# Maxima of the last attention: ScalarE copies half of each bank, VectorE scans both halves together, and a router step of one thread is placed earlier on VectorE

## What is computed

```python
q = jnp.einsum('btd,hdk->bhtk', hidden_states, Wq) + bq[None, :, None, :]
k = jnp.einsum('btd,hdk->bhtk', hidden_states, Wk) + bk[None, :, None, :]
scores = jnp.einsum('bhtk,bhsk->bhts', q, k) * scale
weights = jax.nn.softmax(scores, axis=-1)
out = jnp.einsum('bhts,bhsk->bhtk', weights, v)
```

## Time and profile before

| | |
|---|---|
| runs, median of 3 | 3894.77 us (3893.24 to 3896.06) |
| the profiled execution | 3885.22 us |
| its span | 3883.4 us |
| TensorE matmul, busy | 3146.7 us (81%) |
| VectorE, busy | 2438.9 us (63%) |
| ScalarE, busy | 1662.9 us (43%) |
| GpSimd, busy | 607.5 us (16%) |

### The profile page before, as it was taken

How to read it: one execution, slowest core, us unless ns; L and a number is a source line. 1 busy time by engine, 2 the same in 40 slices (tenths; PEclk the granted TensorE clock), 3 DMA queues, 4 the chain that set the end, 5 groups by cost and what they waited for, 6 DMA issues and landing times.

```text
span 3883.4 us, 43741 instructions
## 1 busy us (share of the span) xinstructions
PE 3146.7 (81%) x16174; PEld 1595.0 (41%) x16174; DVE 2438.9 (63%) x4576; ACT 1662.9 (43%) x2458; POOL 607.5 (16%) x425
## 2 busy tenths in 40 slices
PE   3568769996799868997699868998689977996688
PEld 1134424553245433553245432554235532464145
DVE  4636876478656876568656775568755786534442
ACT  3425515464345624465155634456154642532231
POOL 2001101301022100311023010321013110211030
PEclk8578869998899878998799978998799987997696
DMA  3130244303441243302542152502443124412261
GB/s 111 69 109 1 56 146 127 101 20 100 120 142 48 48 149 109 112 18 73 142 141 69 24 149 70 160 28 54 142 120 104 30 83 133 135 58 62 59 199 46
DMA packets 201351, 355.91 MB, mean 92 GB/s; under 512 B 32994, under 2 KB 124962, under 8 KB 194914
## 3 DMA queue, kind: packets, MB, share of 16 engines
q1 hardware_dynamic: 201137, 353.11, 31.8%
HBM read 302.74 MB, written 49.66 MB: 91 GB/s over the span
## 4 chain that ended last, share of the span: by engine, by line
PE 57%; DVE 23%; DMA 7%; ACT 5%; issue 4%; POOL 2%; SPq 1%; ACTq 0%; DVEq 0%; POOLq 0%
PE PS L1805 6%; DVE MX L1596 6%; PE PS L1828 6%; PE PS L1832 6%; PE PS L1659 5%; PE PS L1667 5%; PE PS L1103 4%; PE PS L1773 3%; DMA UU<-k_scratch 3%; DVE U L898 2%; PE PS L1784 2%; DVE U L891 2%; PE PS L1154 2%; POOL D L1404 2%; PE PS L1238 1%
## 5 line engine op out<-in xcount | busy, mean ns | idle before, releaser
L1404 POOL TENSOR_TENSOR D<-D,GW 128x512 f32<-128x512 f32 x320 | 445.6, 1393 | 1451.7 <-ACT D L1477 1215.6
L783 ACT ACTIVATE U<-U 128x2048 f32<-128x2048 f32 x256 | 487.9, 1909 | 183.2 <-DVE U L891 97.6
L1645 DVE SCALAR_TENSOR_TENSOR D<-D,PS 128x512 f32<-128x512 f32 x336 | 228.4, 680 | 394.8 <-ACT D L1481 279.6
L1477 ACT ACTIVATE D<-PS 128x512 f32<-128x512 f32 x336 | 200.0, 595 | 594.5 <-PE PS L1828 594.5
L1805 PEld LDWEIGHTS PS<-WST,D 128*128 128x128 f32 (+1 forms) x2688 | 354.0, 198 | 173.1 <-DVE D L1650 103.3
L1805 PE MATMUL PS<-WST,D 128*128 128x128 f32 (+1 forms) x2688 | 380.8, 286 | 30.8 <-DVE D L1650 30.6
L1832 PE MATMUL PS<-XT,WST 128*128 128x512 f32 (+1 forms) x672 | 372.8, 637 | 32.5 <-DVE D L1645 31.6
L898 DVE SCALAR_TENSOR_TENSOR U<-PP,RD,QB 128x512 f32<-128x512 f32 x512 | 363.8, 776 | 46.2 <-ACT QB L780 27.4
L1103 PE MATMUL PS<-U,resident 128*32 128x512 f32 x2048 | 302.4, 670 | 104.2 <-ACT U L783 104.2
L1828 PE MATMUL PS<-XT,WST 128*128 128x512 f32 (+1 forms) x672 | 369.7, 633 | 16.8 <-ACT D L1481 10.0
L1596 DVE TENSOR_REDUCE MX<-PS 128x2 f32<-128x1024 f32 x256 | 299.8, 1219 | 114.8 <-PE PS L1751 114.8
(11 more groups left out here) (345 smaller groups left out, 3917.3 us busy)
## 6 DMA issues: line engine op xcount, KB each, us to landing
GW<-gates_scratch SPq DMA_DIRECT2D x320, 256.0 KB, 4.2
WST<-in_pairs_dram SPq DMA_DIRECT2D x336, 192.0 KB, 2.4
U<-band_scratch SPq DMA_DIRECT2D x32, 1280.0 KB, 7.5
UU<-in_w_dram SPq DMA_DIRECT2D x64, 512.0 KB, 7.2
UU<-pad_scratch SPq DMA_DIRECT2D x8, 1792.0 KB
UU<-q_scratch SPq DMA_DIRECT2D x24, 384.0 KB
UU<-k_scratch SPq DMA_DIRECT2D x24, 384.0 KB
e_scratch<-D SPq DMA_DIRECT2D x8, 1024.0 KB, 4.5
```

Of the source, the lines that this page charges most:

```text
L783: e.activation(ring(i), ring(i), ACT.Gelu).then_inc(S["act"], 1)
L1404: e.tensor_tensor(AV[:, n % 3, :], AV[:, n % 3, :], GW[:, p // 2 % GWS, p % 2, :], ALU.mult).then_inc(S["gated"], 1)
```

## The change

Three things change. First, a step of the score pass is one bank and not two, so there are 64. ScalarE copies the upper 256 columns of the bank to SBUF (`MXH`, eight slots). VectorE then runs a `tensor_tensor_scan` with `max` as both operations over the lower 256 columns in PSUM and the copied 256 columns: element i of the result is the maximum of everything up to i in both, and the last element is the maximum of the bank. After four banks (one head) one `tensor_copy` takes the four last elements into `MX3`. Second, the start numbers and `TURN` are new, and with them thread A's L938, L939 and L944 stand earlier on VectorE. Third, the transposes of the gates wait for all 64 scans and not for all but the last step.

```diff
@@ b_act
+            for k in range(64):
+                yield
+                e.wait_ge(S["s1_3"], at("s1_3", b, k + 1))
+                if k == 0:
+                    e.wait_ge(S["q_out3"], at("q_out3", b, 16))
+                    e.wait_ge(S["k_out3"], at("k_out3", b, 32))
+                if k >= 8:
+                    e.wait_ge(S["mx3"], at("mx3", b, k // NT - 1))
+                e.activation(MXH[:, k % 8, :], PZ(k % NT)[:, T // 2:], ACT.Copy).then_inc(S["half3"], 1)
@@ b_dve
-            for k in range(32):
-                yield
-                hd, j = k // 2, 2 * (k % 2)
-                e.wait_ge(S["s1_3"], at("s1_3", b, k + 1))
-                e.tensor_reduce(MX3[:, j:j + 2, hd], PSall[:, 4 + j:6 + j, :], AX.X, ALU.max).then_inc(S["max3"], 1)
-            yield
-            e.wait_ge(S["max3"], at("max3", b, 32))
+            for k in range(64):
+                yield
+                hd, j = k // NT, k % NT
+                e.wait_ge(S["half3"], at("half3", b, k + 1))
+                e.tensor_tensor_scan(MXH[:, k % 8, :], PZ(j)[:, 0:T // 2], MXH[:, k % 8, :], GONE, ALU.max, ALU.max).then_inc(S["max3"], 1)
+                if j == NT - 1:
+                    e.wait_ge(S["max3"], at("max3", b, k + 1))
+                    e.tensor_copy(MX3[:, :, hd], MXH[:, NT * (hd % 2):NT * (hd % 2) + NT, T // 2 - 1]).then_inc(S["mx3"], 1)
+            yield
+            e.wait_ge(S["mx3"], at("mx3", b, NH))
@@ b_pe
-            for k in range(32):
-                yield
-                hd, j = k // 2, 2 * (k % 2)
+            for k in range(64):
+                yield
+                hd, j = k // NT, k % NT
...
-                if k >= 2:
-                    e.wait_ge(S["max3"], at("max3", b, k - 1))
-                for x in range(2):
-                    last = e.matmul(PZ(j + x), QS3[:, hd, P * (j + x):P * (j + x) + P], KS3[:, hd, :], start=True, stop=True)
-                last.then_inc(S["s1_3"], 1)
-            yield
-            e.wait_ge(S["max3"], at("max3", b, 31))
+                if k >= 4:
+                    e.wait_ge(S["max3"], at("max3", b, k - 3))
+                e.matmul(PZ(j), QS3[:, hd, P * j:P * j + P], KS3[:, hd, :], start=True, stop=True).then_inc(S["s1_3"], 1)
+            yield
+            e.wait_ge(S["max3"], at("max3", b, 64))
@@ the table
-TURN = 421.20
+TURN = 412.60
```

More of the change, by code:

```diff
@@ L171, in laid_out @@
     return dict(x=w("L0_attn_x"), consts=packed(CONSTS + MASKS), resident=packed(RESIDENT), passing=packed(PASSING), last=packed(LAST), pairs=wst.reshape(PAIRS, P, 3 * P), w1=w1)
-TURN = 421.20
+TURN = 412.60
 STARTS = {
     "a_act": (
[8 rows of a table removed]
[8 rows of a table added]
     ),
     "a_dve": (
[9 rows of a table removed]
[9 rows of a table added]
     ),
     "a_pe": (
[11 rows of a table removed]
[11 rows of a table added]
     ),
     "a_pool": (
-        1.68, 20.05, 273.64,
+        1.68, 20.05, 265.09,
     ),
     "a_sp": (
-        -63.22, 192.47, 196.99, 211.93, 212.85, 213.79, 214.73, 215.98, 216.90, 217.84, 228.00, 239.84, 286.01, 288.83, 290.63, 297.73,
-        302.12, 351.97,
+        -63.22, 193.21, 197.74, 207.85, 208.18, 208.52, 208.85, 216.94, 217.27, 217.61, 225.91, 234.66, 277.46, 280.27, 282.07, 289.18,
+        293.57, 343.38,
     ),
     "b_act": (
[13 rows of a table removed]
[17 rows of a table added]
     ),
     "b_dve": (
[14 rows of a table removed]
[16 rows of a table added]
     ),
     "b_pe": (
[23 rows of a table removed]
[25 rows of a table added]
     ),
     "b_pool": (
[3 rows of a table removed]
[3 rows of a table added]
     ),
     "b_sp": (
[6 rows of a table removed]
[6 rows of a table added]
     ),
@@ L448, in build @@
         SPL3 = D3[:, 2 * T:5 * T].bitcast(BF16).rearrange("p (a k t) -> p a k t", a=2, k=3)
+        MXH = D3[:, 0:4 * T].rearrange("p (s t) -> p s t", s=8)
         PT3 = D3[:, :].rearrange("p (s t) -> p s t", s=8)
```

## The result

| | before | changed |
|---|---|---|
| median of the runs | 3891.66 us (3882.89 to 3896.06, 14 runs) | 3901.39 us (3896.12 to 3908.85, 14 runs) |
| ratio | | 1.003, 95% interval 1.0022 to 1.0037 |
| the profiled execution | 3885.22 us | 3902.40 us |
| its span | 3883.4 us | 3900.6 us |

The change made the kernel slower by 0.3%, some 12 us on 3891. The forecast had the sign and the mechanism, but 42 us of loss. Some 3 us of the distance to 3937 us come from the base: the median of the kernel before is 3891.66 us over 14 runs, where three had given 3894.77. A second comparison of the same two kernels gave 1.0043 (1.003 to 1.0056).

What follows compares the result with a forecast made beforehand. VectorE's score pass was taken as the bound. Seven turns at 4.2 + 0.86 = 5.1 us (35.7) plus 6.3 in the last made 42 us on 3885.2, or 3927; 9.6 more for the median gave 3937 us, range 3887 to 3968.

Steps and rivals of the forecast that it cites:

- The scan's duration: Score pass on VectorE: a scan over 256 column pairs takes two steps per element, 512 steps, 680 ns.
- The head: Score pass on VectorE: four scans and a small copy take 2.74 us; sixteen heads 43.9 us against 37.6 for reduces.
- The gaps: VectorE's idle times in a middle score pass, around thread A's groups on TensorE: 3.5 us together, against 5.6 before.
- The router step: L938 and L939 moved between L1044 and L1046 on VectorE: L1046 and L1048 start 0.86 us later in seven turns.
- A microsecond more in the pass is a microsecond more in the turn: Score pass: everything after it waits, so its growth, 4.2 us in a middle pass, counts in full.
- The full-rate scan: Rival, chance 0.14: a scan runs at one element per step, 419 ns; 3875 us with TensorE's lower clock bounding the pass.
- My other price: Score pass with scans at one element per step and TensorE's upper clock throughout: middle pass 38.2 us, kernel 3833 us.
- The hidden scan: Rival, chance 0.05: scans are slow but gaps shrink by VectorE's added work, path over the DMAs; around 3895 us.
- The later load from k_scratch: Rival: earlier band stores delay this load by 2 us a turn, giving 3951 us; no separate chance, inside main case's range.

Runs made afterwards that it cites:

- experiment 5: Changed kernel with scans over 128 pairs of columns in place of 256, half the columns left out of the maxima; 3815.44 us in a single execution.
- experiment 2: Kernel before with only thread A's three router operations moved ahead on VectorE, reduces of pairs kept; two runs: 3891.32 us (0.9999) and 3891.33 us (1.000).
- experiment 4: Changed kernel with each scan replaced by a plain tensor_tensor max over the same operands, maxima of two columns only; 3821.20 us, ratio 0.9821 to the kernel before.
- the single reduces: Changed kernel with scans, ScalarE's copies and small copies replaced by one tensor_reduce per 512-column bank; 3878.36 us (0.9961), or 3875.83 us (0.996) with router steps back.
- kernels of the table: Kernel before (3891.66 us), changed (3901.39), changed with router operations put back (3894.14, 3894.02), and that with one reduce a bank instead of scans (3875.83).
- experiment 6: Changed kernel without ScalarE's copies, scans waiting for the matmul alone, upper half of each bank left out of the maxima; 3891.07 us, ratio 1.0003 to the kernel before.

## Why the prediction had the sign and not the size

*The scan's duration: right.* 680 ns was forecast and 669 measured, with the count of steps given: two steps of 1.02 ns for each pair of columns (experiment 5). The Trainium skill's rule of half throughput (the page "DVE: opcode table, instruction layouts, handler registers and perf-mode slots", section "Datapath and trigger behaviour") holds in this trace: 2.05 ns for each column of a scan, 1.06 for each column of a reduce.

*The head: the term that was mis-sized.* I let scans overlap by 0.044 us, the figure of the reduces of pairs, and let the small copy cost 0.156. Measured, the overlap is 0.082 and the copy costs 0.12: 0.04 of waiting and 0.08 until the next scan. A head is 2.54 us and not 2.74, a pass of 16 heads 40.6 and not 43.9. That is 3.2 us in each of eight passes, 26 us of the 30 that the forecast has too much. The last turn shows it alone: +6.3 us forecast, 40.7 - 37.6 = +3.1 measured. I took the overlap from the one group in which the instructions are twice as long and TensorE at its lower level paces them (experiment 2). The right one stood in other rows of the kernel before, such as two of L1025, whose mean of 0.419 us I did use: they start 0.75 - 0.419 = 0.331 us apart, an overlap of 0.088. Even the earlier trace rows has seven reduces of pairs in 8.01 us, 1.13 us apart, in a stretch in which the granted clock was 0.96.

```profile
2080.03 0.75 DVE L1025 TENSOR_TENSOR LO<-PS,resident 128x256 f32<-128x256 f32 x2 [2.44 <-PE PS L1268]
```

One bank or half of one per instruction has it at 0.08 with three different operations: 0.082 for the scans, 0.085 for the plain operation of experiment 4 ((1.41 - 0.416) / 3 = 0.331 apart), 0.078 for the single reduces.

*The gaps: near.* Forecast 3.5 us with the scans, measured 4.15 as a mean over the seven turns (4.2 in the second profile). So the middle pass grew by 1.9 us and not by 4.2: 3.2 less for the heads, 0.6 to 0.8 more for the gaps. That the copy makes the gaps longer is shown, and so is that its busy time is hidden, as forecast (experiment 6).

*The router step: right in the split, unclear in the time.* The delay of 0.86 us is 0.94, and against the kernel before the stretch from the end of the split to the first maximum doesn't shrink. Beside the scans its undoing gives 9 to 11 us, for 6 us forecast. Beside reduces of pairs it costs nothing that can be measured, and the forecast's 0.15% is outside both intervals; beside reduces of single banks the intervals are too wide to tell. What takes it up there is not settled; beside pairs the clock level of TensorE in the pass differs between the profiles (experiment 2) and is one candidate.

*What I left out.* "A microsecond more in the pass is a microsecond more in the turn" is not quite so. The two stretches behind the pass are shorter with all kernels of the table that have one bank per step, in the changed kernel by 0.5 and 0.8 us a turn, 9 us in all. In the first of them the transposed products of thread A (L1168, now L1177) take less time, here in the fourth turn before and after:

```profile
1921.69 3.62 PE L1168 MATMUL PS<-resident,QE 128*128 128x128 f32 x16
```

```profile
1934.02 2.84 PE L1177 MATMUL PS<-resident,QE 128*128 128x128 f32 x16
```

The granted clock of the stretch between the pass and thread A's update rose from 0.51 to 0.58 in this turn. This fits a TensorE that reaches its upper level sooner, but no experiment took that apart. It isn't the size of the step alone: the kernel of experiment 4 has one bank per step too and takes 11.4 and 272.8 us for the two stretches, hardly less than the kernel before. The cause of these 9 us stays open.

The sum of the profiles: 7 x 1.9 + 3.1 for the passes and 7 x 0.94 for the split are 23 us, less 9 behind the pass: 14 us. The two comparisons gave 12 and 17 us (0.3% and 0.43%). Against the 42 us of the forecast, the heads take off 26 us and the stretches behind the pass 9, and the gaps add some 5.

*The rivals.* The full-rate scan is out (experiment 5), and its main price was wrong as well: I let TensorE bound it at its lower clock level. Experiment 4 shows 3821 us and not 3875, with a granted clock of 0.95 in the last pass. My other price, 3833 us with the upper level throughout, was near: 38.2 us for a middle pass and 38.5 measured. The hidden scan is nearest to the measured size, but not by its mechanism: the work on VectorE grew and stayed on the path. The later load from k_scratch is out; the stretch is 21.6 us before and after.

## What to carry to other kernels

Before an operation with a running result is put in the place of a reduction, count its steps for each element: a scan over two halves cost as much as a reduce over the whole (669 ns against 678), and the copy on another engine that prepared it bought nothing. The gain lay beside it: a bank at a time, four in flight, with the old operation and the new places of thread A's steps was 0.4% faster than pairs. And take the overlap of instructions from rows of the same length: an error of 0.04 us, repeated 512 times on the path, was most of the error of this forecast (some 20 of 30 us).

## What the hardware showed that I had not expected

TensorE's clock level differed within one kind of work. 64 score matmuls, one every 0.634 us, had a granted clock of 0.54 over a pass of 40.7 us, and the same 64, one every 0.386 us, had 0.95 over 25.0 us (experiment 4). In both passes TensorE waited for VectorE before nearly every matmul, 32.0 and 17.6 us in 60 waits. A bound worked out from the lower level (four matmuls in 2.16 us) therefore forbade a speed that was reached (a head in 1.53 us).

How closely the matmuls stand doesn't settle the level alone. The last pass of the kernel before and that of experiment 2 have the same matmuls and orders, and nearly the same rhythm, but a granted clock of 0.55 and 0.87. The reduces of pairs were paced by the level: 1.175 us apart while TensorE was at the lower one, 1.13 at the upper.
